# Experts stage of a perceiver block on one core: rows turned a quarter ahead, first weights prepared in the gate's part, bias rows made among the first rounds

## What is computed

```
x = transpose(hidden_states, (1, 0, 2))
h = relu(einsum('bsh,oh->bso', x, gW1) + gb1)
gate = einsum('bsh,eh->bse', h, gW2) + gb2
g = gate.mean(axis=1)
W1 = einsum('be,eoi->boi', g, eW1)
b1 = g @ eb1
W2 = einsum('be,eoi->boi', g, eW2)
b2 = g @ eb2
y = relu(einsum('bsi,boi->bso', x, W1) + b1[:, None, :])
y = einsum('bsi,boi->bso', y, W2) + b2[:, None, :]
```

## Time and profile before

| what | value |
|---|---|
| median of the runs | 2803.23 us (2801.91 to 2805.48, 3 runs) |
| the profiled execution | 2813.74 us |
| its span in the profile | 2811.9 us |
| mean granted TensorE clock | 0.966 |
| PE busy | 2535.6 us, 90% |
| DVE busy | 1788.0 us, 64% |
| ACT busy | 1212.2 us, 43% |
| POOL busy | 1811.1 us, 64% |
| chain that ended last | PE 9%, DVE 3%, all other 0 to 1% (followed back to the last stage) |

### The profile page before, as it was taken

How to read it: one execution, slowest core, us unless ns; L and a number is a source line. 1 busy time by engine, 2 the same in 40 slices (tenths; PEclk the granted TensorE clock), 3 DMA queues, 4 the chain that set the end, 5 groups by cost and what they waited for, 6 DMA issues and landing times. The chain is left out here.

```text
span 2811.9 us, 58861 instructions
## 1 busy us (share of the span) xinstructions
PE 2535.6 (90%) x23620; PEld 1557.9 (55%) x23620; DVE 1788.0 (64%) x3165; ACT 1212.2 (43%) x2017; POOL 1811.1 (64%) x1481
## 2 busy tenths in 40 slices
PE   5999999999999999999999999999464777679998
PEld 4666666656565665666666566655332221446666
DVE  5666666665666666666666666665274899446665
ACT  3433334333333333334333333333165688146665
POOL 5777677777776777777777777775122688245553
PEclk9999999999999999999999999999787999889999
DMA  7788888887888877788888878887400000011111
GB/s 204 173 172 183 170 174 176 177 170 175 177 170 168 171 181 171 168 185 172 177 180 175 171 165 186 173 188 147 103 0 0 12 1 1 26 54 55 55 55 48
DMA packets 1061424, 373.37 MB, mean 133 GB/s; under 512 B 983744, under 2 KB 1031488, under 8 KB 1061024
## 3 DMA queue, kind: packets, MB, share of 16 engines
q1 hardware_dynamic: 1061152, 369.61, 60.9%
HBM read 122.02 MB, written 4.19 MB: 45 GB/s over the span
## 5 line engine op out<-in xcount | busy, mean ns | idle before, releaser
L392 POOL TENSOR_TENSOR pl<-prob,ph 128x1601 f16<-128x1601 f32 x256 | 826.8, 3230 | 511.2 <-DVE ph L681 287.4
L427 PE MATMUL psum<-yT,Q 128*128 128x512 f16 (+1 forms) x5120 | 921.6, 335 | 24.4 <-ACT prob L585 22.1
L585 ACT ACTIVATE prob<-psum,nb 128x1601 f32<-128x1601 f32 x256 | 408.8, 1597 | 1058.8 <-DVE nb L674 771.5
L444 PE MATMUL psum<-yN,hT 128*128 128x384 f16 (+1 forms) x3328 | 836.9, 326 | 2.5 <-DMA lT<-pl 1.8
L445 PE MATMUL psum<-yN,lT 128*128 128x192 f16 (+1 forms) x3328 | 814.7, 246 | 0.0
L427 PEld LDWEIGHTS psum<-yT,Q 128*128 128x128 f16 x5120 | 438.1, 98 | 504.8 <-ACT prob L585 33.4
L681 DVE CAST ph<-prob 128x1601 f16<-128x1601 f32 x256 | 295.5, 1154 | 483.9 <-ACT prob L585 469.5
L672 DVE TENSOR_REDUCE mx<-psum 128x1 f32<-128x1024 f32 (+1 forms) x512 | 502.7, 990 | 101.3 <-PE psum L427 94.1
L444 PEld LDWEIGHTS psum<-yN,hT 128*128 128x128 f16 (+1 forms) x3328 | 325.3, 98 | 202.0 <-issue 2.1
L445 PEld LDWEIGHTS psum<-yN,lT 128*128 128x128 f16 (+1 forms) x3328 | 326.0, 98 | 0.0
L1635 DVE COPY W<-psum 128x1024 f32<-128x1024 f32 x128 | 156.8, 1225 | 117.9 <-PE psum L1510 116.6
(11 more groups left out here) (165 smaller groups left out, 3069.7 us busy)
## 6 DMA issues: line engine op xcount, KB each, us to landing
stage<-in_ctxN SPq DMA_DIRECT2D x96, 384.0 KB
wnat<-in_WF SPq DMA_DIRECT2D x32, 512.0 KB, 4.1
stage<-in_ctxT SPq DMA_DIRECT2D x32, 400.5 KB
stage<-in_ctxT SPq DMA_DIRECT2D x64, 200.2 KB
stage<-in_ctxT SPq DMA_DIRECT2D x32, 400.0 KB
stage<-in_ctxT SPq DMA_DIRECT2D x64, 200.0 KB
hT<-ph SPq DMA_TRANSPOSE x256, 3.7
lT<-pl SPq DMA_TRANSPOSE x256, 3.3
```

What stands on the lines that cost most here:

```text
L392: pool.tensor_tensor(pl[:, 0:J], prob[:, :], ph[:, 0:J], ALU.subtract).then_inc(lo_kept, 1)
L427: ins = pe.matmul(psS[:, lo:hi], Q[p % 2][:, q, b, tt * P:(tt + 1) * P], yT[b][:, y, lo:hi], start=(n == 0), stop=(n == 4))
L444: pe.matmul(psO[:, 0:2 * CTX], hT[G % 2][0:k, n, :], yN[b][0:k, n, :], start=(n == 0), stop=False)
L585: act.activation(prob[:, :], psS[:, 0:J], ACT.Exp, bias=nb[:, G % 2:G % 2 + 1], scale=SCALE, accum_out=den[:, G % 4:G % 4 + 1]).then_inc(e ...
```

## The change

Three things are done, all in `experts`.

1. PE turns groups 0 to 3 first (two quarters), then makes quarter 0's matmuls, turns groups 4 and 5, makes quarter 1's, turns 6 and 7, makes quarters 2 and 3. ACT copies groups 0 to 3, then makes the relus of a quarter before the copies of the groups turned behind it.
2. The first weight group's two halves are turned, copied and cut in the gate's part: `turn_weights(0, 0)` stands behind the last gate matmul and ahead of the small one, `turn_weights(0, 1)` behind it, `keep_rows` behind ACT's last relu, `cut` behind POOL's columns. The functions are moved outward for that, and take the engine as an argument.
3. The three `Gexp` operations go from the end of the gate's part to DVE's queue in the rounds' part, one behind each copy of rounds 0, 1 and 2. They have a semaphore of their own (`g_rows`), for which PE waits ahead of its first `apply1`. `first`, `ghi` and `glo` keep their memory in both parts.

```diff
@@ in the gate's part: POOL @@
                 for st in range(2):
                     make_columns(pool, st)
+                for j in range(2):
+                    cut(pool, 0, j)
@@ DVE @@
-                for q, cut in enumerate((ghi, glo, ghi)):
-                    rows = slice(32 * q, 32 * q + 32)
-                    dve.tensor_scalar(Gexp[rows, :, :], cut[rows, :][:, :, None].to_broadcast([32, T, B]), first[rows, 0:1], None,
-                                      ALU.mult).then_inc(g_step, 1)
@@ PE @@
-                for g in range(NPAIR // 2):
+
+                for g in range(4):
                     ln.turn(pe, g)
-                    if g % 2 == 0:
-                        continue
-                    c = g // 2
-                    pe.wait_ge(ln.kept, g + 1)
+                for c in range(4):
+                    pe.wait_ge(ln.kept, 2 * c + 2)
                     if c == 0:
                         pe.wait_ge(w_small, 16 * 13)
                     for m in range(2):
...
                         ins.then_inc(gate_h, 1)
+                    if c < 2:
+                        ln.turn(pe, 2 * c + 4)
+                        ln.turn(pe, 2 * c + 5)
+                turn_weights(pe, 0, 0)
                 pe.wait_ge(gate_sum, 8)
                 pe.wait_ge(wide, 2)
                 for m in range(2):
                     ins = pe.matmul(psum[:, 1024:1024 + T], gW2w[:, m, :], hs[:, m, :], start=(m == 0), stop=(m == 1))
                 ins.then_inc(g_mm, 1)
+                turn_weights(pe, 0, 1)
@@ ACT @@
-                ln.keep(act, 0)
-                ln.keep(act, 1)
+                for g in range(4):
+                    ln.keep(act, g)
                 act.wait_ge(w_small, 16 * 13)
-                for c in range(1, 4):
-                    ln.keep(act, 2 * c)
-                    ln.keep(act, 2 * c + 1)
-                    relu(2 * c - 2)
-                    relu(2 * c - 1)
+                for c in range(3):
+                    relu(2 * c)
+                    relu(2 * c + 1)
+                    if c < 2:
+                        ln.keep(act, 2 * c + 4)
+                        ln.keep(act, 2 * c + 5)
                 relu(6)
                 relu(7)
+                for j in range(2):
+                    keep_rows(act, 0, j)
@@ in the rounds' part: POOL @@
             for st in range(NST):
-                for j in range(2):
-                    cut(st, j)
+                for j in range(2 if st else 0):
+                    cut(pool, st, j)
                 if st + 2 < NST:
                     make_columns(pool, st + 2)
@@ PE @@
             def apply1(ob, q):
                 G, r = divmod(q, 4)
+                if ob == q == 0:
+                    pe.wait_ge(g_rows, 3)
...
-            turn_weights(0, 0)
-            turn_weights(0, 1)
@@ ACT @@
-            keep_rows(0, 0)
-            keep_rows(0, 1)
@@ DVE @@
+            def gate_rows(q):
+                rows = slice(32 * q, 32 * q + 32)
+                dve.tensor_scalar(Gexp[rows, :, :], (ghi, glo, ghi)[q][rows, :][:, :, None].to_broadcast([32, T, B]),
+                                  first[rows, 0:1], None, ALU.mult).then_inc(g_rows, 1)
+
...
                         keep_mixed(st, v)
+                    if half == 0 and k < 3:
+                        gate_rows(k)
```

More of the change, by code:

```diff
@@ L1270, in experts @@
         eb2s = sb("eb2s", [P, C], F16)
+        first = sb("first", [P, 4])
+        ghi = sb("ghi", [P, T], F16)
+        glo = sb("glo", [P, T], F16)
         wnat_in = [sem(f"wnat_in{n}") for n in range(2)]
@@ L1284, in experts @@
         g_step = sem("g_step")
+        g_rows = sem("g_rows")
         mixed = sem("mixed")
@@ L1304, in make_columns, with cut, turn_weights, keep_rows @@
                                  nat[:, u // 2, u % 2]).then_inc(col_made, 1)
+        psW = bank(psum, 4)
+        def cut(pool, st, j):
+            n = 2 * st + j
+            pool.wait_ge(row_kept, n + 1)
+            if st >= 2 and j == 0:
+                pool.wait_ge(mixed, 4 * (st - 1))
+            hi, lo = (v[st % 2][:, 4 * j:4 * j + 4, :].rearrange("p (k u) n -> p k (u n)", k=2) for v in (whi, wlo))
+            pool.tensor_copy(hi, wrow).then_inc(hi_cut, 1)
+            pool.wait_ge(hi_cut, n + 1)
+            pool.tensor_tensor(lo, wrow, hi, ALU.subtract).then_inc(lo_cut, 1)
+        def turn_weights(pe, st, j):
+            n = 2 * st + j
+            pe.wait_ge(col_made, 8 * st + 4 * j + 4)
+            if n:
+                pe.wait_ge(row_kept, n)
+            for u in range(4):
+                ins = pe.transpose(psW[:, u * P:(u + 1) * P], wcol[st % 2][:, 4 * j + u, :], ident[:, :])
+            ins.then_inc(w_turned, 1)
+        def keep_rows(act, st, j):
+            n = 2 * st + j
+            act.wait_ge(w_turned, n + 1)
+            if n:
+                act.wait_ge(lo_cut, n)
+            act.activation(wrow, psW.rearrange("p (k n) -> p k n", k=2), ACT.Copy).then_inc(row_kept, 1)
         with ExitStack() as cs:
@@ L1310, in experts @@
             gb2 = sbs("gb2", [P, 1])
-            first = sbs("first", [P, 4])
             hs = sbs("hs", [P, 2, T])
             g32 = sbs("g32", [P, T])
-            ghi = sbs("ghi", [P, T], F16)
-            glo = sbs("glo", [P, T], F16)
             wide = sem("wide")
@@ L1443, in mix_psum @@
             return psum[:, 1024 * (n % 2):1024 * (n % 2) + 1024]
-        psW = bank(psum, 4)
         def apply_bank(n):
@@ L1490, in _ @@
         def _(pe):
[L1491 to L1498, removed]
             def mix(st, v):
@@ L1574, in _ @@
                         if v % 2 == 0 and st + 1 < NST:
-                            turn_weights(st + 1, v // 2)
+                            turn_weights(pe, st + 1, v // 2)
                     if second:
@@ L1590, in _ @@
         def _(act):
[L1591 to L1594, removed]
-                    act.wait_ge(lo_cut, n)
-                act.activation(wrow, psW.rearrange("p (k n) -> p k n", k=2), ACT.Copy).then_inc(row_kept, 1)
             def keep_mixed(st, v):
@@ L1620, in _ @@
                         if v % 2 == 0 and st + 1 < NST:
-                            keep_rows(st + 1, v // 2)
+                            keep_rows(act, st + 1, v // 2)
                     if second:
```

## The result

| | before | changed |
|---|---|---|
| median, 6 runs each | 2803.63 us (2801.24 to 2806.94) | 2792.34 us (2789.22 to 2797.07) |
| ratio, 95% interval | | 0.9958 (0.9946 to 0.9970) |
| profiled execution: span | 2811.9 us | 2795.3 us |
| its mean granted TensorE clock | 0.966 | 0.967 |

The change saves 11.3 us by the medians; the forecast was 9.3 us and 2793.9 us. Of the 16.6 us between the two spans, 4.3 lie ahead of the gate's first row transpose (2442.28 us before, 2437.95 now), where the code didn't change: the executions simply differ there. From that transpose to the end of the span it was 369.62 us and is 357.35, 12.3 less.

A forecast was written before the change was run, and what follows sets the result against it. PE's waits in the gate, the serial hand-over and DVE's copies in the first rounds were taken as the bound. 4.6 + 5.4 - 0.4 - 0.3 = 9.3 us saved, from 2803.23 to 2793.9 us; range 2789.5 to 2799.0.

The forecast's parts named there:

- term one: In the gate: turning rows one quarter ahead removes PE's waits before the matmuls, saving 4.6 us (3.3 to 5.9).
- term three: In the first rounds: three Gexp operations behind DVE's copies cost 0.3 us, with bounds of 0 and 2.4 us.
- Term two: In the gate's tail: the first round starts 5.4 us earlier, less 0.4 us for POOL and DVE hindering each other.
- the rival on the port: In the first rounds: all three Gexp meet POOL's work, each 0.8 us late; gain 7.2 us, 2796.0 us; chance 15%.
- The wait for g_rows: In the rounds: PE's new wait never holds, since PE reads Gexp first in round 9, over 20 us on.
- POOL's wait for the third group's load: In the rounds: it delays POOL's cut of group 1, with 2.7 us to spare; costed at nothing, bound 0.8 us.
- The gate's waits: Rival in the gate: the removed waits return elsewhere, leaving a gain of 4.7 us, 2798.5 us; chance 8%.
- The clock rose in the gate: Rival in the gate: the clock doesn't rise there, 10.1 us lost against 4.7 won, 2808.6 us; chance 3%.
- The first rounds: Rival in the first eight rounds: full clock there saves 3.1 us more, 2790.8 us; chance 10%.

The follow-up runs named there:

- the third trace: The changed kernel, unedited, traced a third time: 20.58 us from PE's first row transpose of the gate to the small gate matmul; ratio 0.9960 to the kernel before.
- the second pair of traces: The kernel before and the changed kernel, each traced again without an edit: 368.09 and 357.30 us from the gate's first row transpose to the span's end.

## Why the prediction was right, step by step

The time fell within the range, in the direction and by the mechanism forecast: the waits went, the first weights ran under the gate's tail, and the bias rows found room in the rounds. It fell by 2 us more than the sum. The gain of term one was put 2.1 us too low and the cost of term three 1.2 us too low, and it is luck that these two partly cancel.

**Term one, quarters ahead: forecast 4.6 us (3.3 to 5.9), measured 6.7.** This is the mis-sized term, and it left its own bounds. Up to the turning behind quarter 0 I had expected 0.7 us more than before, for the two turns that moved there less the hole that they fill. The traces have 0.87 us less (8.23 and 7.36), though PE makes eight more transposes in it. Of these 1.6 us, 1.2 are the clock's rise, after 4.4 us instead of 6.8. That was named as a bound (1.3 us) and left out of the sum, as if an earlier rise were no likelier than a later one; the traces with the new order (3.4 to 5.0 us) and the old (6.8 to 8.4) show that it goes with the order. With 1.2 us more the term would be 5.8 and still within its bounds. What took it out of them is the idle time. From there to the small matmul it was 5.33 us by my reading (4.29 of waits and 1.04 of the moved turns) and 5.86 by the traces. The idle times in brackets begin at the modelled end of a matmul, and where nothing is waited for the next group starts 0.16 us before that end (2441.42 + 4.05 = 2445.47, and the transposes start at 2445.31). So each wait was worth some 0.15 us more than its row said. The 0.4 us of the first part that the clock doesn't explain may be the same at the first hole; it wasn't tested apart.

**Term two, first weights and bias rows out of the gate's tail: forecast 5.4 less 0.4 for the port, measured 5.29.** The order of ends came as worked out: POOL last, DVE 1.7 us earlier, PE's turnings hidden. The meeting of POOL and DVE went mostly to DVE's harmless side (`ghi` 0.67 us in place of 0.20), and POOL's cast lost 0.2 us (0.82 in place of 0.61) instead of 0.4.

**Term three, bias rows in the rounds: forecast 0.3, measured 1.5 in two traces (1.2 in the third), most of it the clock.** Of the three operations one met the port and the other two were free. Its 1.28 us grew by 0.37. In the third trace, where round 3 ran at the low clock throughout, the room that the forecast saw there (0.35 us) nearly held that, and DVE came 0.06 us late. In the first, the clock rose during the round; less the 0.43 us by which DVE was late it would have been 2.5 us, as long as round 7 was before (2.52). Either way it took 2.94, in place of 2.82 before. So the rival on the port, all three late, was too much, and one in three was right. Its price was too high as well: where a Gexp met the whole subtraction, the round was 0.6 us longer (3.46 and 3.50 us) and not 0.8, since 0.2 us of it can run beside.

The rest is the clock, for which the term has nothing. In stage c it is the 0.37 us of round 7 (2.52 before, 2.89 after), and it goes on behind the border at round 8: rounds 8 and 9, which end up in d, ran at 2.26 us before and still partly at the low clock now. From the first copy of DVE to the one of round 10 it was 25.90 and 25.92 us before and is 27.45, 27.49 and 27.14. Whether a shorter hand-over makes the clock rise later among the rounds, or by chance it was so in these executions, no run settles.

**What was costed at nothing.** The wait for g_rows never showed. POOL's wait for the third group's load (4.71 us) and the cut behind it had room in the changed kernel at the low clock, as forecast; PE's run at full clock used it up.

**The rivals.** The gate's waits didn't come back. The clock rose in the gate, sooner and not later. The first rounds ran mostly at the low clock, as forecast, and the run that kept PE at work shows that rival's price: c 19.76 in place of 22.5. (That rival's sum took the bias rows off twice, once in the forecast and once in the 0.84 us; it should have read 3.4 us more and 2790.5.)

**The sum.** 6.73 + 5.29 - 1.55 = 10.5 us up to the copy of round 10, and 10.4 in the second pair of traces. Behind it the code is the same, and the pairs differ by another 1.9 and 0.4 us: 12.3 and 10.8 in all, with 1 us of the first the accident of round 11. The medians have 11.3.

## What to carry to other kernels

Where PE waits for a copy that another engine makes behind other work, moving the producer one step ahead removes the wait. Here the clock also rose some 3 us sooner with the new order, so look at the granted clock in the stretch where the work moves, and take it into the sum. Work taken off a serial tail is won in full only up to the next engine's end, so work out the ends of all engines before the barrier (here 2.1 and 4.3 us alone, 5.3 together). Before placing DVE work beside POOL's, look which operations stretch each other, and put them where POOL waits for a load.

## What the hardware showed that I had not expected

The granted clock was partly repeatable. In two executions each of both kernels it rose in the gate at the same distance from PE's first transpose to within 0.2 us (6.8 and 6.8 before, 4.4 and 4.5 changed). But a third execution of the changed kernel had 3.4, and the fall ahead of the gate came 5.9, 9.1 and 6.9 us before that transpose in the three. What the order of PE's work moved was the range: 6.8 to 8.4 us in five traces, 3.4 to 5.0 in six.

PE's work of no use (transposes of the identity, 0.11 us each) held the clock at 2.4 GHz as well as real work, across a wait of 10 us and a hand-over of 3.7. And a fall can come after the rest that goes ahead of it: with a rest of 2.4 us the clock fell 1.3 us after PE had started again, and the low stretch of 3.4 us cost the gate as much as if PE had not been kept busy at all (21.03 against 21.08 us).

DVE's Gexp and POOL's subtraction took turns in both directions, with the same remainder each time: 1.08 us for the Gexp behind the subtraction, 1.01 us for the subtraction behind the Gexp.
